# Interleaving neighbouring score and weight products in TensorE's order, with two repairs of the norm on GpSimd

## The reference, cut to what matters

```python
def _ln(x):
    mu = jnp.mean(x, axis=-1, keepdims=True)
    var = jnp.var(x, axis=-1, keepdims=True)
    return (x - mu) * jax.lax.rsqrt(var + LN_EPS)
...
attn_w = jax.nn.softmax(jnp.einsum('bhqd,bhkd->bhqk', q, k) * scale, axis=-1)
attn_out = jnp.einsum('bhqk,bhkd->bhqd', attn_w, v)
...
scores = jnp.einsum('bqhd,bkhd->bhqk', q, k) / jnp.sqrt(jnp.float32(D))
top_s, top_i = jax.lax.top_k(scores, TOPK)      # TOPK = 16, the last attention
attn = jax.nn.softmax(top_s, axis=-1)
```

## Time and profile before

| what | value |
|---|---|
| median of 3 runs | 673.63 us (669.01 to 683.54) |
| the profiled execution, its time | 665.29 us |
| its span, first to last instruction | 663.5 us |
| mean granted TensorE clock | 0.863 |

### The profile page before, as it was taken

One profiled execution on the slowest core, in us unless ns is written; L12 is line 12 of the kernel. 1 busy time (PEld: TensorE's weight loads), 2 busy tenths in 40 slices (PEclk: granted clock), 3 DMA queues, 4 the chain that ended last, 5 costly groups with the idle time before them and its releaser, 6 DMA issues.

```text
span 663.5 us, 14489 instructions
## 1 busy us (share of the span) xinstructions
PE 570.0 (86%) x5152; PEld 378.9 (57%) x5152; DVE 490.9 (74%) x1291; ACT 386.3 (58%) x669; POOL 306.4 (46%) x584
## 2 busy tenths in 40 slices
PE   3888989899999999999998889786999987867477
PEld 3645556566756565657665556554655664634246
DVE  2577767853859687745377727999999999999953
ACT  2546878799696887886757766452233531611133
POOL 6884535435845444364562446641341446111133
PEclk9858999999999999998989979777575795765779
DMA  9560344302333533020335043140020002000000
GB/s 319 143 159 3 88 106 112 73 2 54 76 67 69 105 77 78 2 65 2 66 72 123 2 129 68 28 101 0 2 65 2 2 10 64 9 1 2 1 2 16
DMA packets 15062, 39.23 MB, mean 59 GB/s; under 512 B 2641, under 2 KB 6801, under 8 KB 14737
## 3 DMA queue, kind: packets, MB, share of 16 engines
q0 software_dynamic: 8960, 29.37, 20.1%
q1 hardware_dynamic: 5312, 8.46, 3.8%
q10 hardware_dynamic: 720, 0.49, 0.3%
HBM read 7.96 MB, written 0.52 MB: 13 GB/s over the span
## 4 chain that ended last, share of the span: by engine, by line
DVE 38%; PE 37%; ACT 8%; DMA 6%; issue 6%; POOL 4%; ACTq 0%; POOLq 0%
PE psum L1590 10%; DVE left L1419 8%; DVE left L1429 7%; DVE top L1426 6%; DVE top L1416 6%; DVE maxima L1406 5%; PE psum L1566 5%; PE psum L1536 5%; ACT softmax_T L1298 4%; DMA qk_stack<-centred 3%; PE psum L1625 3%; PE psum L1636 3%; DMA qk_stack<-qk_parts 2%; DVE maxima L1402 2%; PE psum L1617 2%
## 5 line engine op out<-in xcount | busy, mean ns | idle before, releaser
L1298 ACT ACTIVATE softmax_T<-psum 128x1024 f32<-128x1024 f32 (+1 forms) x224 | 210.9, 962 | 111.7 <-PE psum L1577 73.3
L1406 DVE TENSOR_REDUCE maxima<-psum 128x4 f32<-128x1024 f32 x160 | 190.1, 1216 | 52.4 <-PE psum L1536 51.6
L1566 PE MATMUL psum<-qk_stack 32*128 32x256 f32 (+1 forms) x896 | 114.9, 346 | 28.1 <-DMA qk_stack<-centred 9.6
L1590 PE MATMUL psum<-softmax_T,values 128*32 128x256 f32 (+1 forms) x1792 | 129.9, 408 | 4.8 <-ACT softmax_T L1298 3.5
L1566 PEld LDWEIGHTS psum<-qk_stack 32*128 32x128 f32 x896 | 72.3, 202 | 71.0 <-issue 31.0
L1227 POOL TENSOR_SCALAR unpicked<-left 128x512 bf16<-128x512 f32 x64 | 39.5, 616 | 136.0 <-DVE left L1429 135.3
L1536 PE MATMUL psum<-qk_stack 32*128 32x256 f32 (+1 forms) x768 | 89.6, 335 | 9.2 <-ACT softmax_T L1298 2.4
L1536 PEld LDWEIGHTS psum<-qk_stack 32*128 32x128 f32 x768 | 58.9, 200 | 37.5 <-issue 16.5
L1590 PEld LDWEIGHTS psum<-softmax_T,values 128*32 128x32 f32 x1792 | 56.7, 118 | 40.3 <-issue 12.0
L1187 POOL TENSOR_TENSOR qk_parts<-qk_parts 128x256 fp32r<-128x256 f32 x56 | 40.9, 730 | 77.0 <-ACT qk_parts L1281 76.6
L1158 POOL DMA_DIRECT2D qk_stack<-qk_parts x112 | 63.7, 580 | 7.0 <-POOL qk_parts L1187 6.3
(11 more groups left out here) (99 smaller groups left out, 870.3 us busy)
## 6 DMA issues: line engine op xcount, KB each, us to landing
qk_stack<-qk_parts POOLq DMA_DIRECT2D x112, 256.0 KB, 5.1
weights<-in_w SPq DMA_DIRECT2D x1, 1408.0 KB, 13.5
row_biases<-in_rows SPq DMA_DIRECT2D x1, 1088.0 KB, 10.8
weights<-in_w SPq DMA_DIRECT2D x2, 512.0 KB, 5.9
weights<-in_w SPq DMA_DIRECT2D x1, 832.0 KB, 9.0
qk_stack<-centred SPq DMA_DIRECT2D x48, 8.0 KB
weights<-in_w SPq DMA_DIRECT2D x1, 768.0 KB, 4.3
weights<-in_w SPq DMA_DIRECT2D x1, 576.0 KB, 3.7
```

The source lines that it names most:

```text
L1298: nc.scalar.activation(pT[:, slot, u % 2, :, 0:cols].rearrange("p (i t) n -> p i t n", t=NT), two_banks(step).rearrange("p i (t n) -> p i ...
L1406: nc.vector.tensor_reduce(rows[:, u // 4, u // 2 % 2, g:g + 2, :], ps.rearrange("p i (t k) -> p i t k", t=NT), AX_X, ALU.max).then_inc(fin, 1)
L1566: ins = nc.tensor.matmul(ps[:, i, t, 0:P if window else N], QKS[b][32 * g:32 * g + 32, s, 1, P * t:P * t + P], QKS[b][32 * g:32 * g + 32, ...
L1590: ins = nc.tensor.matmul(misc[32 * g:32 * g + 32, queries], V[:, b, t, first:first + 32], pT[:, slot, g // 2, 2 * (g % 2) + t, 0:P if wind ...
```

## The change

Three edits.

1. **Interleaving.** The planner's order stays as it is, step for step, and so do the banks. The planner also notes for each step when it could have started (`could`). Two neighbours in TensorE's list that both are full `scores`, full or window `weights` or `topk`, that use different row groups, and of which the second could have started, by the plan, no later than 0.15 us after the first did, are written as one: all waits of both, then the first half (t = 0) of each, then the second half (t = 1) of each. That makes 59 pairs. Of these 48 join a scores with a weights step, 6 are two scores steps, 4 are two weights steps, and the last joins a topk step with a weights step of the window layer. None of the 59 pairs stands later than 411 us in the trace of before.
2. **The first norm.** GpSimd's wait for `k_rows` moves from ahead of the first step to the first `stack`, the first step that uses it.
3. **The negated mean.** `neg_mean` is dropped from all 48 `z` steps. The centring passes subtract the mean instead of adding the negated one.

```diff
+WOVEN_WITH = {}
+for _a, _b in zip(ORDERS["pe"], ORDERS["pe"][1:]):
+    if (weaves(_a) and weaves(_b) and _a not in WOVEN_WITH.values() and not row_groups(_a) & row_groups(_b)
+            and _b not in SPARE and COULD["pe", _b] <= TIMES["pe", _a][0] + 0.15):
+        WOVEN_WITH[_a] = _b
...
-            pool.wait_ge(k_rows_s, 16 * SLOTS["qk"])
+            first_stack = next(i for i, s in enumerate(ORDERS["pool"]) if s[0] == "stack")
             for step in ORDERS["pool"]:
...
+                    if step == ORDERS["pool"][first_stack]:
+                        pool.wait_ge(k_rows_s, 16 * SLOTS["qk"])
...
-                    nc.gpsimd.tensor_scalar(nmean[:, b, c, :], mv[:, b, c, :, 0], -1.0, 0.0, ALU.mult, ALU.add)
                     link(nc.gpsimd.tensor_scalar(veps[:, b, c, :], mv[:, b, c, :, 1], 1.0, eps, ALU.mult, ALU.add))
...
-                        ins = nc.gpsimd.tensor_scalar(dst[:, b, t, :], src[:, b, t, :], nmean[:, b, c, t:t + 1],
-                                                      rstd[:, b, c, t:t + 1], ALU.add, ALU.mult)
+                        ins = nc.gpsimd.tensor_scalar(dst[:, b, t, :], src[:, b, t, :], mv[:, b, c, t, 0:1],
+                                                      rstd[:, b, c, t:t + 1], ALU.subtract, ALU.mult)
...
+            def half(step, t):
+
+                kind, b, l, u = step
+                if kind == "topk":
...
+                s, ps = u // 2, two_banks(step)
+                own, other = (1, 0) if kind == "weights" else (0, 1)
+                moving = slice(P * t, P * t + P) if ATTN[l]["kind"] == "window" else slice(0, N)
+                for j in range(2):
+                    g = 2 * (u % 2) + j
+                    ins = nc.tensor.matmul(ps[:, j, t * N:t * N + moving.stop - moving.start],
+                                           QKS[b][32 * g:32 * g + 32, s, own, P * t:P * t + P],
+                                           QKS[b][32 * g:32 * g + 32, s, other, moving], start=True, stop=True)
+                return ins
...
             for step in ORDERS["pe"]:
+                if step in WOVEN_WITH.values():
+                    continue
...
+                if weaves(step):
+                    inputs_in(step)
+                    if step in WOVEN_WITH:
+                        other = WOVEN_WITH[step]
+                        banks_free(pe, other)
+                        inputs_in(other)
+                        half(step, 0)
+                        half(other, 0)
+                        half(step, 1).then_inc(fin, 1)
+                        half(other, 1).then_inc(done[other[0], "pe"], 1)
+                    else:
+                        half(step, 0)
+                        half(step, 1).then_inc(fin, 1)
```

More of the change, by code:

```diff
@@ L571, with weaves @@
 }
+def weaves(step):
+    kind, b, l, u = step
+    if kind == "topk":
+        return True
+    return kind == "scores" and ATTN[l]["kind"] == "full" or kind == "weights" and ATTN[l]["kind"] != "topk"
 def w_group(blk):
@@ L782, in plan @@
     lists = {e: [] for e in engines}
-    clock, spare = Clock(), {}
+    clock, spare, could = Clock(), {}, {}
     table, last, queue = "exp", 0, 16.0
@@ L870, in plan @@
         taken = choose(t)[1]
+        could[t] = max([ready_at[t]] + [when for _, which in taken for when, _, _ in which])
         d, lag = busy(t), 0.0
@@ L916, in plan @@
         left -= 1
-    return lists, slot, had, done, spare
+    return lists, slot, had, done, spare, could
 def _sorted(order, deps):
@@ L961, with row_groups @@
         [1.3, 1.4, 437.2, -0.3, 0.9, -1.2, 4.4, 87.9, 52.7, -9.6]]
-ORDERS, SLOT, HAD, TIMES, SPARE = plan(LEAD, landed)
+ORDERS, SLOT, HAD, TIMES, SPARE, COULD = plan(LEAD, landed)
+def row_groups(step):
+    return {step[3] % 4} if step[0] == "topk" else {2 * (step[3] % 2), 2 * (step[3] % 2) + 1}
+WOVEN_WITH = {}
[3 more added lines that the diff above has]
+        WOVEN_WITH[_a] = _b
 NTH = {}
@@ L1463, in _, with inputs_in @@
             seen = set()
+            def inputs_in(step):
+                kind, b, l, u = step
+                if kind == "weights":
+                    pe.wait_ge(max_in[b], maxima_count(l, u // 2 if ATTN[l]["kind"] == "topk" else u // 4))
+                elif kind == "topk":
+                    pe.wait_ge(stacked[b][u // 4], 16 * (l + 1))
+                else:
+                    pe.wait_ge(stacked[b][u // 2], 16 * (l + 1))
+            def half(step, t):
+                kind, b, l, u = step
+                if kind == "topk":
+                    s, g = u // 4, u % 4
+                    return nc.tensor.matmul(bank(step)[:, N * t:N * t + N], QKS[b][32 * g:32 * g + 32, s, 0, P * t:P * t + P],
+                                            QKS[b][32 * g:32 * g + 32, s, 1, :], start=True, stop=True)
+                s, ps = u // 2, two_banks(step)
[7 more added lines that the diff above has]
+                return ins
             pe.wait_ge(ident_s, 16)
@@ L1558, in _ @@
                     s = u // 2
-                    window, topk = ATTN[l]["kind"] == "window", ATTN[l]["kind"] == "topk"
                     ps = two_banks(step).rearrange("p i (t n) -> p i t n", t=NT)
-                    pe.wait_ge(max_in[b], maxima_count(l, s if topk else s // 2))
+                    inputs_in(step)
                     for t in range(NT):
-                        queries = slice(P * t, P * t + P) if window else slice(0, N)
                         for i in range(2):
                             g = 2 * (u % 2) + i
[L1566 to L1579, removed]
+                            nc.tensor.matmul(ps[:, i, t, :], QKS[b][32 * g:32 * g + 32, s, 1, P * t:P * t + P],
+                                             QKS[b][32 * g:32 * g + 32, s, 0, :], start=(t == 0), stop=False)
@@ new lines, in _ @@
+                    pe.wait_ge(consts_s, 3)
+                    for i in range(2):
+                        after(pe, "pool", ("topk", b, l, 2 * u + i))
+                        for t in range(NT):
+                            for r in range(NT):
+                                ins = nc.tensor.matmul(ps[:, i, t, P * r:P * r + P],
+                                                       unpicked[:, 4 * SLOT["picks", ("topk", b, l, 4 * s)][0] + 2 * (u % 2) + i, r, P * t:P * t + P], drop[:],
+                                                       start=False, stop=(t == 1 and r == 1))
```

22 lines of the change are left out of this document (6 added, 16 removed).

## The result

The changed kernel has a median of 679.15 us (20 runs, 669.65 to 691.76), the kernel before 671.12 us (20 runs, 660.4 to 683.54). The ratio is 1.0141, with a 95% interval of 1.0099 to 1.0183: the change costs 8.0 us by the medians and 9.5 us by the ratio. The forecast was a gain of 2.4 us, 671 us with a range of 662 to 679. The sign was wrong, and the median lies just outside the range. Ratios in this document leave out the executions that are over 1.5% above the fastest of their kernel; medians and means are over all executions.

The account below looks back on a forecast made before the run. TensorE or a batch's latency was taken to bound the kernel until about 410 us, then VectorE in the top-k layer. Terms 0 + 0.5 - 2.0 - 0.9 = -2.4 us from a 673.63 median gave 671 us, range 662 to 679.

Parts of the forecast that it names:

- The negated mean: GpSimd's norms: dropping 48 neg_mean instructions shortens four later norms on the chain; -0.9 us, ends -1.3 and -0.3.
- the first norm: First layer on GpSimd: the norm starts at about 7.0 us, the first stack's DMAs at about 18.0; -2.0 us.
- the early start is given back: Rival: a DMA or the slow clock at 28 us absorbs the first layer's 2.0 us; 673 us, chance 0.10.
- What is late next: At the four later norms on the chain, mostly the same batch's own transposes; so -0.9 taken of 1.0 us.
- The interleaving's gain of 0: TensorE's 59 pairs: neighbouring steps already run beside each other, so nothing is won; at most 1.3 us from issue gaps.
- The pair of the earlier trace: First the pair at 76.88 us, taking 0.45 us unchanged; under held steps the one at 65.67, held by 0.72 us.
- The rival of program order: Rival: TensorE matmuls really keep program order, so each of 59 pairs saves 0.22 us; 658 us, chance 0.07.
- The held first steps: TensorE pairs: a first step waits until its partner is ready, delaying its reader; +0.5 us, from 0 to 4.2.
- the cover: Pair at 65.67 us: ScalarE's 0.89 us of idle time ahead of its copy at 68.12 absorbs the 0.72 us hold.
- the rival 678: Rival: uncovered holds of first steps decide and the kernel gets slower, by +4.3 us; 678 us, chance 0.13.
- The clock: Rival: an earlier start shifts the clock's rise after the slow stretch from 28 to 56 us; 668 or 674, chance 0.15.

Follow-up runs that it names:

- e6: The changed kernel with one word put back, centring passes adding the mean instead of subtracting it (computes another norm): median 668.81 us, ratio 0.9971 to the kernel before.
- e2: The kernel before with only the negated mean dropped and the mean subtracted where it lies: median 676.12 us, ratio 1.0073.
- e7: The kernel before with the mean edit and the later wait for k_rows, without interleaving: median 672.19 us, ratio 1.0085.
- e3: The kernel before with only the later wait for k_rows: median 668.31 us, ratio 0.9873.
- a1: The whole changed kernel measured again, against the kernel before: median 680.05 us, ratio 1.0145.
- e4: The kernel before with the 59 interleaved pairs and the later wait, negated mean and addition kept: median 673.53 us, ratio 1.0108.
- a3: The kernel before with only the later wait for k_rows, measured again in another group: median 666.78 us, ratio 1.0027.
- a4: The kernel before with the 59 interleaved pairs and the later wait, measured again: median 673.07 us, ratio 1.0069.
- e1: The kernel before with only the 59 interleaved pairs: median 673.87 us against 672.63 beside it, ratio 0.9977.
- e8: The kernel before with the later wait and 111 interleaved pairs, steps ready up to 0.6 us apart by the plan: median 678.77 us, ratio 1.0235.
- e5: The kernel before with neg_mean made the plain mean in its own tile and the passes subtracting it: one execution, 683.80 us; a pass takes 794 ns.

## Why the prediction was wrong, and where it was right

**The step that failed** is the sentence "Subtraction in place of addition, and the mean read where it lies, have the same form and size; I take 0 for both, with a bound of 0.05 us by 8 norms, 0.4 us". The mean read where it lies does cost next to nothing (8 ns, e6). The subtraction costs 350 ns a pass, 0.70 us a norm, fourteen times the bound. With it the mean edit costs 3.5 to 6.5 us (e2, e7 against e3, a1 against e4), where the forecast had a gain of 0.9. The trace of before had no row of this operation, and the bound was set by likeness of shape, not by rows of other operations. With an upper end of twice the pass, 0.9 us a norm by the same 8 norms, it would have been 7 us, and the case of a slower kernel one to be weighed.

**The negated mean** (-0.9) and **the first norm** (-2.0) turned with it. The start at 7.05 us and, with short passes, the first stack at 18.08 (e3), 18.52 (a3) and 18.40 (e6) are as worked out, and a3 and e3 are 3.7 and 4.3 us faster in the median; the term was right in mechanism, and in size within what the clock leaves open. In the changed kernel four norms of 2.75 us gave all of it back. That the early start is given back was a rival (673, 0.10), but by a DMA or the clock; it was given back on GpSimd itself.

**"What is late next"** was read from a trace with norms of 2.2 us, most of which were hidden. The forecast took it that a norm that is off the chain stays off. Eight more came onto it, in places where TensorE had been the chain (158 to 166 us). An engine at 46% is hidden only as far as each of its steps is, and here a batch's norm stands between two stretches of its TensorE work.

**The interleaving's gain of 0** was right. The pair of the earlier trace rows in the trace of after, PE alone:

```profile
76.59 0.51 PE L1509 MATMUL psum<-qk_stack 32*128 32x256 f32 x8
77.03 0.38 PE L1666 MATMUL psum<-gated_projection,normed_T 128*128 128x128 f32 x1
```

0.44 us for two steps, as against 0.45 before: what the new order writes down TensorE had done by itself. The rival of program order (658, 0.07) is out. With it goes, for this kernel, the rule of the Trainium skill's page "TensorE: Matmul & The Clock Gate", Part 3, "The mechanism", that matmuls start in program order: the trace of before has the later step's first matmuls at 76.89 us, ahead of two of the earlier step at 77.11.

**The held first steps** are a real cost, sized too low by most of the runs. The pair of the earlier trace rows is held as forecast, both steps behind the later wait:

```profile
65.97 0.74 PE L1509 MATMUL psum<-qk_stack 32*128 32x256 f32 x12 [1.00 <-DVE maxima L1428]
...
66.51 1.02 ACT L1320 ACTIVATE softmax_T<-psum 128x1024 f32<-128x1024 f32 x1 [1.13 <-PE psum L1509]
66.55 3.56 DVE L1428 TENSOR_REDUCE maxima<-psum 128x4 f32<-128x1024 f32 x3 [0.84 <-PE psum L1509]
...
67.83 0.38 ACT L1332 ACTIVATE mixed_T<-psum 128x256 f32<-128x256 f32 x1 [0.29 <-PE psum L1639]
```

ScalarE and VectorE both wait for the one start here; for VectorE, whose scores were the later step, that is nothing new. ScalarE's copy has 0.29 us of idle time ahead of it in place of 0.89: the cover held, as forecast. Where the scores are the step that is held, VectorE can be left without work. At a pair of scores and weights of after, VectorE's run over the blocks breaks off for 0.72 us:

```profile
235.12 1.19 DVE L1428 TENSOR_REDUCE maxima<-psum 128x4 f32<-128x1024 f32 x1
...
236.50 0.73 PE L1509 MATMUL psum<-qk_stack 32*128 32x256 f32 x12 [0.41 <-ACT mixed_T L1332]
237.03 4.62 DVE L1428 TENSOR_REDUCE maxima<-psum 128x4 f32<-128x1024 f32 x4 [0.72 <-PE psum L1509]
```

The same place of before. The scores step (L1536) starts while VectorE is still reading the blocks ahead, and the run has no gap until its next wait, 0.42 us ahead of 237.17:

```profile
233.15 3.60 DVE L1406 TENSOR_REDUCE maxima<-psum 128x4 f32<-128x1024 f32 x3
...
233.95 0.40 PE L1536 MATMUL psum<-qk_stack 32*128 32x256 f32 x4
```

The term was +0.5 with an upper end of 4.2, and the rival 678 stood at 0.13. Measured, it is 5.6 +- 1.9 us on top of the wait edit (a4 against a3), and +1.2 in the median alone (e1), where it can't be told from 0; e6 shows none of it. The cover was judged at one place, ScalarE's 0.89 us of idle time, and for the scores step of the pair at 236.50 there is none. How much of a4's 5.6 is holds and how much is the clock stays open: by the fit in the last section some 3.6 of it go with more time at the lower level, 209 us against 198, and 2.0 are left, an estimate that the upper end of 4.2 would cover. For e8, whose time at the lower level is about a3's (201 us), some 11 of the 11.9 us are left. So that held steps cost time is shown by the 111 pairs; what the 59 cost is not settled beyond some 0 to 6 us. The forecast also called ScalarE and VectorE near their limits until 285 us; its own rows have them busy for 110.1 and 95.5 of 135 us.

**The clock** as a rival (0.15) did not decide the median: the two profiles have 0.860 and 0.863, and e5 and e6 show the cause without it. It goes with much of the spread. The forecast's reading of its fall was loose: the granted clock is 1.00 until 28 us, with TensorE busy for 14.9 of the last 18 us, and just around the fall TensorE is idle for 1.42 us, a wait that ends with a copy of ScalarE (`context_T`).

The sum by what was measured: the mean edit on top of the wait 3.9 us (e7 against e3, medians), the wait -3.7 to -4.3, the interleaving on top of the wait 5.2 to 6.3 (medians of e4 and a4): together 5 to 6.5 us, where the whole change has 8.0 by its medians. The rest lies within the error of sums of four medians. How the loss divides between subtraction and interleaving depends on the order in which they are added: from e3 (of another group) over e6 to a1 it is 0.5 us for the interleaving with the dropped `neg_mean`, and then 11.2 for the subtraction. The fastest version is the kernel before with the later wait alone, 668.31 and 666.78 us in two groups.

## What to carry over

An operation that is swapped for "the same with another sign" is a new operation until a row shows its duration: look for one in the trace, and where there is none, bound it by a whole further pass and not by likeness. A repair that drops 48 small instructions can be right and still lose through the one that it changes; here the one-word run (e6) would have been the first thing to measure. Writing down an order that the engine already finds by itself won nothing here, and joining the waits of two steps makes the earlier one as late as the later, so join only steps that are ready together or whose readers have other work.

## What the runs showed of the chip beyond that

- GpSimd's `tensor_scalar` on 128x128 f32 with two operands per partition takes 447 ns as add and multiply and 794 to 797 ns as subtract and multiply (e5 and the changed kernel). Its form with two tensors does not show this: a subtraction on 128x256 took 732 ns (L1209, fp32r out), an addition of that size 727 ns (L1241, f32 out).
- TensorE starts matmuls of a later step ahead of matmuls that stand before them, when they use other row groups: at 76.89 us, ahead of two at 77.11. Two steps of four take 0.45 us together, one alone 0.44.
- Executions of one kernel differ by their clock. Over the 29 executions of the kernel before in the first group, each further us at the lower level (1.2 GHz, from the mean granted clock) goes with 0.31 us of time, and over the 20 of the changed kernel with 0.34 (a straight-line fit, an estimate; the other kernels with 12 executions or more give 0.22 to 0.41). It doesn't say which is cause and which effect. Two executions of the changed kernel in one stretch, the profiled one above and that of a1 (span 681.0 us), by windows:

```profile
120.00:156.00 36.00, 31.70 (x344) 20.60 (x342) 20.67 (x36) 29.86 (x47) 13.78 (x21) 1.00 0.12 29
```

```profile
120.00:156.00 36.00, 32.77 (x295) 19.51 (x291) 22.61 (x37) 23.83 (x36) 14.79 (x23) 0.76 0.14 32
```

The third column from the right is the granted clock. At 0.76 TensorE gets through 295 matmuls in these 36 us in place of 344, with more busy time. e2 and e3 have such a stretch at the same place (0.76 and 0.81) and before, in its profile, has not. One profile against another would have put that down to the change.
